# A four-layer Mamba and FFN stack: kernel products of the mixer in adjacent pairs, its output weights loaded a slot ahead, and the closing stage laid out over other banks and engines

## What is computed

```python
# layer 3, per group g of 8, 16 heads of 64 channels, chunks of 128 tokens
M      = einsum('bcihn,bcjhn->bcijh', C, B) * exp(segsum(A*dt))   # 128 x 128 kernels per head
y      = M @ (hid*dt) + (part from the chunk before) + D*hid
yg     = y * silu(gate)
yg     = yg * rsqrt(mean(yg*yg over the group) + eps) * gnorm_w
out    = yg @ out_proj_w.T                                         # 8192 -> 512
# layer 4, blocks of 128, FP8_MAX = 448
def act_quant(x): s = max(|x|)/448 + 1e-12 per token and block; return x/s, s
g, u   = quantised(x) @ w1.T, quantised(x) @ w3.T                  # 512 -> 1792
y      = quantised(silu(g)*u) @ w2.T                               # 1792 -> 512
```

## Time and profile before

| | |
|---|---|
| median of 3 runs | 3027.28 us |
| profiled execution | 3027.26 us |
| its span | 3025.4 us |
| PE busy | 2543.9 us (84%) |
| DVE busy | 1906.6 us (63%) |
| POOL busy | 1276.6 us (42%) |
| ACT busy | 1165.5 us (39%) |
| granted TensorE clock, mean | 0.939 of full |

### The profile page before, as it was taken

The page is one execution under the profiler, slowest core; times in us unless marked ns, Lnnn a source line. Parts: engine busy times, 40 slices in busy tenths (PEclk is TensorE's granted clock), DMA queues, the critical chain, the costliest instruction groups (busy, mean ns, idle before and its releaser), DMA issues. The chain is left out here.

```text
span 3025.4 us, 37783 instructions
## 1 busy us (share of the span) xinstructions
PE 2543.9 (84%) x12700; PEld 1817.9 (60%) x12700; DVE 1906.6 (63%) x2968; ACT 1165.5 (39%) x1935; POOL 1276.6 (42%) x914
## 2 busy tenths in 40 slices
PE   6846667655716999999999999999999999878997
PEld 5611112114615777777777777777777777567886
DVE  4439999985254664565564554655655655487877
ACT  2264444432113553453543543543544534431111
POOL 2109989971002553442543534533534524442212
PEclk9959999997758999999999999999999999889999
DMA  2021030000131110100110100100100101111010
GB/s 72 19 71 43 0 111 0 0 28 28 39 129 54 44 44 23 44 30 23 44 37 16 55 26 23 51 29 23 51 23 24 50 23 37 34 53 39 26 43 29
DMA packets 47743, 116.00 MB, mean 38 GB/s; under 512 B 6560, under 2 KB 6944, under 8 KB 46560
## 3 DMA queue, kind: packets, MB, share of 16 engines
q1 hardware_dynamic: 47584, 113.91, 11.7%
HBM read 104.32 MB, written 9.57 MB: 38 GB/s over the span
## 5 line engine op out<-in xcount | busy, mean ns | idle before, releaser
L1203 POOL TENSOR_TENSOR mg_y<-mg_hT,mg_sg 128x512 f32<-128x512 f32 x128 | 165.4, 1292 | 808.0 <-DVE mg_hT L1453 808.0
L78 PE MATMUL mg_pb<-xT2h,mg_wh 128*128 128x512 f32 x1152 | 464.9, 404 | 15.3 <-POOL mg_wl L1193 15.3
L79 PE MATMUL mg_pb<-xT2l,mg_wh 128*128 128x512 f32 x1152 | 452.5, 393 | 0.0
L80 PE MATMUL mg_pb<-xT2h,mg_wl 128*128 128x512 f32 x1152 | 450.0, 391 | 0.0
L1574 ACT ACTIVATE mg_gb<-mg_gb 128x384 f32<-128x384 f32 x512 | 219.6, 471 | 476.1 <-PE mg_gb L1298 475.9
L743 PE MATMUL ss_y<-ss_pr,cst 128*128 128x512 f32 x512 | 293.2, 661 | 126.4 <-POOL ss_pr L728 116.1
L728 POOL TENSOR_TENSOR ss_pr<-ss_h,ss_bc 128x512 f32<-128x512 f32 x256 | 328.4, 1287 | 38.3 <-DVE ss_h L696 28.5
L1422 DVE SCALAR_TENSOR_TENSOR mg_hT<-mg_pb,mg_cw,mg_hT 128x510 f32<-128x510 f32 (+2 forms) x432 | 318.2, 738 | 34.3 <-ACT mg_hT L1552 32.8
L1446 DVE TENSOR_TENSOR mg_m<-mg_gb,mg_cb 128x384 f32<-128x384 f32 x512 | 270.6, 550 | 43.5 <-ACT mg_gb L1574 33.4
L743 PEld LDWEIGHTS ss_y<-ss_pr,cst 128*128 128x128 f32 x512 | 80.3, 193 | 337.8 <-POOL ss_pr L728 329.4
L78 PEld LDWEIGHTS mg_pb<-xT2h,mg_wh 128*128 128x128 f32 x1152 | 216.8, 188 | 74.3 <-issue 34.9
(11 more groups left out here) (287 smaller groups left out, 5358.5 us busy)
## 6 DMA issues: line engine op xcount, KB each, us to landing
mg_ws<-in_w_in SPq DMA_DIRECT2D x72, 512.0 KB, 3.5
ss_bc<-bc_rows SPq DMA_DIRECT2D x16, 1024.0 KB, 8.8
mg_wos<-in_w_out SPq DMA_DIRECT2D x64, 256.0 KB, 2.6
mg_lr<-acs_rows SPq DMA_DIRECT2D x512, 4.0 KB
ff_ws<-in_w SPq DMA_DIRECT2D x7, 1024.0 KB, 5.0
x<-in_x SPq DMA_DIRECT2D x16, 256.0 KB, 4.1
ip_ws<-in_w_in SPq DMA_DIRECT2D x8, 512.0 KB, 3.3
x_kept<-x SPq DMA_DIRECT2D x2, 2048.0 KB, 7.2
```

Of the source, the lines that this page charges most:

```text
L78: pe.matmul(out, lhs[0], rhs[0], start=start, stop=False)
L79: pe.matmul(out, lhs[0], rhs[1], start=False, stop=False)
L80: return pe.matmul(out, lhs[1], rhs[0], start=False, stop=stop)
L1203: pool.tensor_tensor(yb[:, p % RING, t], hT[s % 2][:, t], sg[s % 2][:, t], ALU.mult).then_inc(s_y2, 1)
```

## The change

In the mixer:
- The landing tile of output weights is doubled (`mg_wos0`, `mg_wos1`), each with its semaphore, and SP issues the loads of slot s+1 at the end of slot s, after the second row loads.
- ScalarE makes the first high weight right after exponential 1 and the second after exponential 5; it copies the high half of the second output tile before exponentials 6 and 7.
- VectorE's products 2 and 3, and 4 and 5, stand next to each other. The low half of the first output tile moves behind the second dt product, that of the second tile ahead of the first skip; the low weights stand ahead of the second dt product and after the last tap of the second half.

In the closing stage:
- Output tiles go to four banks, those of `ff_po` and `ff_pg`; x is transposed into two banks of its own (`tl_px`), three tiles behind the output matmuls instead of two, so that the last three transposes fall in the first three FFN items.
- The scaling of chunk 0's weights moves from GpSimd to ScalarE, as 24 activations of 128 columns; the rounding copies of all chunks are ScalarE's, for chunk f+1 in item 4 of chunk f. GpSimd keeps the subtractions, now in six pieces of 512 columns for each chunk.
- The two broadcast multiplies of `product` become two scalings of 128 columns with two scalars each.

The diff, cut to its core:

```diff
@@ mixer: SP
-                    for w in new_out_weights(s) if s < NSTEP else []:
-                        if w:
-                            sp.wait_ge(s_wgl, w)
-                        sp.dma_start(wos[:], I["w_out1"][w]).then_inc(s_wo, 16)
                     if s == NSTEP:
                         break
                     if more:
                         load_rows(p + 1, 1)
+                    for w in new_out_weights(s + 1):
+                        if w >= 2:
+                            sp.wait_ge(s_wgl, w - 1)
+                        sp.dma_start(wos[w % 2][:], I["w_out1"][w]).then_inc(s_wo[w % 2], 16)
@@ mixer: VectorE
                         kernel_of(p, 1)
+                        if ow:
+                            low_weight(ow[0])
+                        times_step(p, 1)
                         if outs:
                             low(*outs[0])
-                        times_step(p, 1)
                         tap(1, s, 0)
                         kernel_of(p, 2)
+                        kernel_of(p, 3)
                         tap(2, s, 0)
-                        kernel_of(p, 3)
                         tap(3, s, 0)
-                        if ow:
-                            low_weight(ow[0])
                         tap(1, s, 1)
                         kernel_of(p, 4)
+                        kernel_of(p, 5)
                         tap(2, s, 1)
-                        kernel_of(p, 5)
                         tap(3, s, 1)
+                        if ow:
+                            low_weight(ow[1])
                         if outs:
                             add(*outs[0])
+                            low(*outs[1])
                         skip(p, 0)
...
@@ mixer: ScalarE
                             high(*outs[0])
+                        if ow:
+                            high_weight(ow[0])
                         first_tap(s, 0)
                         decay(p, 2)
                         decay(p, 3)
-                        if ow:
-                            high_weight(ow[0])
                         first_tap(s, 1)
                         decay(p, 4)
                         decay(p, 5)
+                        if ow:
+                            high_weight(ow[1])
                         if bc:
                             first_tap(s, 2)
+                        if outs:
+                            high(*outs[1])
                         decay(p, 6)
                         decay(p, 7)
...
@@ closing stage: banks
-        ob = banks(c, "tl_ob", 2)
+        px = banks(c, "tl_px", 2)
         pg = banks(c, "ff_pg", 2)
         pt = banks(c, "ff_pt", 2)
         po = banks(c, "ff_po", 2)
+        ob = po + pg
@@ closing stage: GpSimd
-                scaled(pool, 0, 0)
-                scaled(pool, 0, 1)
-                scaled(pool, 0, 2)
+                def low_part(f, part, piece):
+                    hi_w, lo_w, src = (wh, wl, ws) if part < 2 else (w2h, w2l, w2s)
+                    k = (2 * piece, 2 * piece + 2) if part < 2 else (piece, piece + 1)
+                    pick = (lambda t: t[:, part, k[0]:k[1]]) if part < 2 else (lambda t: t[:, k[0]:k[1]])
+                    i = pool.tensor_tensor(pick(lo_w[f % 2]), pick(src), pick(hi_w[f % 2]).bitcast(F32), ALU.subtract)
+                    if part and piece:
+                        i.then_inc(s_lo, 1)
...
                     add_x(m)
+                    if 2 <= m < 5:
+                        pool.wait_ge(s_hi, 2)
+                        low_part(0, m - 2, 0)
+                        low_part(0, m - 2, 1)
...
+                    for part in range(3):
+                        low_part(f, part, 0)
+                        low_part(f, part, 1)
@@ closing stage: TensorE
-                    if m >= 2:
-                        turn_x(m - 2)
...
+                    if m >= LAG:
+                        turn_x(m - LAG)
+                for n in range(ITEMS):
                     gate_up(n)
+                    if n < LAG:
+                        turn_x(MT - LAG + n)
+                    if n >= 1:
+                        turn_h(n - 1)
+                    if n >= 2:
+                        down(n - 2)
@@ closing stage: ScalarE
+                def scale_up(part):
+                    if part == 0:
+                        act.wait_ge(s_w, 64)
+                    wv, scv = chunk_blocks(0, part)
+                    for b in range(2 * KD):
+                        i = act.activation(wv[:, b], wv[:, b], ACT.Copy, scale=scv[:, b:b + 1])
+                    i.then_inc(s_dq, 1)
+
+                def weights_high(f):
+                    act.wait_ge(s_dq, f * 3 + 3)
+                    if f == 1:
+                        act.wait_ge(s_out, Y0 + MT)
+                    if f >= 2:
+                        act.wait_ge(s_o, (f - 1) * MT)
+                    act.activation(wh[f % 2], ws[:], ACT.Copy).then_inc(s_hi, 1)
+                    act.activation(w2h[f % 2], w2s[:], ACT.Copy).then_inc(s_hi, 1)
+
                 high(0)
                 high(1)
+                scale_up(0)
...
+                    norm_o(m)
+                    if m < 2:
+                        scale_up(m + 1)
+                    if m == 2:
+                        weights_high(0)
+                    if m >= LAG:
+                        x_high(m - LAG)
+                root(1, MT - 1, MT)
+                for n in range(ITEMS):
+                    f, m = divmod(n, MT)
                     silu(n)
+                    if n < LAG:
+                        x_high(MT - LAG + n)
+                    if n >= 1:
+                        h_high(n - 1)
+                    if m == 4 and f + 1 < FC:
+                        weights_high(f + 1)
@@ closing stage: VectorE
-                    ch.link(dve.tensor_tensor(hv, hv, qr[i][:].unsqueeze(2).to_broadcast([P, 2, QB]), ALU.mult))
-                    dve.tensor_tensor(hv, hv, qs[i][:].unsqueeze(2).to_broadcast([P, 2, QB]), ALU.mult
-                                      ).then_inc(s_h, 1)
+                    for b in range(2):
+                        ins = dve.tensor_scalar(hv[:, b], hv[:, b], qr[i][:, b:b + 1], qs[i][:, b:b + 1],
+                                                ALU.mult, ALU.mult)
+                    ins.then_inc(s_h, 1)
...
+                stats_x(MT - 1)
                 for n in range(ITEMS):
                     f, m = divmod(n, MT)
                     product(n)
+                    if n == 0:
+                        quantised(MT - 1)
                     if n >= 1:
                         h_low(n - 1)
                     if n >= 2:
                         add(n - 2)
+                    if n < LAG:
+                        x_low(MT - LAG + n)
```

More of the change, by code:

```diff
@@ L1091, in mixer_groups @@
         wl = [sb(c, f"mg_wl{i}", [P, KD, 2 * P], F32R) for i in range(2)]
-        wos = sb(c, "mg_wos", [P, DM])
+        wos = [sb(c, f"mg_wos{i}", [P, DM]) for i in range(2)]
         yh = sb(c, "mg_yh", [P, PAIRS, P], F32R)
@@ L1514, in _ @@
                         kernel_of(p, 7)
-                        if ow:
-                            low_weight(ow[1])
                         if outs:
-                            low(*outs[1])
                             add(*outs[1])
@@ L1585, in high_weight @@
                 def high_weight(w):
-                    act.wait_ge(s_wo, 16 * w + 16)
+                    act.wait_ge(s_wo[w % 2], 16 * (w // 2) + 16)
                     if w >= PAIRS:
                         act.wait_ge(s_out, w // PAIRS * MT)
-                    act.activation(wogh[:, w % PAIRS, :], wos[:], ACT.Copy, scale=gn[:, w:w + 1]).then_inc(s_wog, 1)
+                    act.activation(wogh[:, w % PAIRS, :], wos[w % 2][:], ACT.Copy, scale=gn[:, w:w + 1]).then_inc(s_wog, 1)
                 def root(g):
@@ L1810, in out_tile @@
                     pe.wait_ge(s_yl, Y0 + m + 1) if m < 2 else pe.wait_ge(s_ylp, m - 1)
-                    if m >= 2:
-                        pe.wait_ge(s_acc, Y0 + m - 1)
+                    if m >= 4:
+                        pe.wait_ge(s_acc, Y0 + m - 3)
                     for k in range(PAIRS):
-                        last = mm3(pe, ob[m % 2][:], (yh[m % 2][:, k, :], yl[m % 2][:, k, :]),
+                        last = mm3(pe, ob[m % 4][:], (yh[m % 2][:, k, :], yl[m % 2][:, k, :]),
                                    (wogh[:, k, :], wogl[:, k, :]), k == 0, k == PAIRS - 1)
@@ L1822, in turn_x @@
                     for k in range(KD):
-                        last = pe.transpose(pt[m % 2][:, k * P:(k + 1) * P], acc[:, m, k * P:(k + 1) * P], ident)
+                        last = pe.transpose(px[m % 2][:, k * P:(k + 1) * P], acc[:, m, k * P:(k + 1) * P], ident)
                     last.then_inc(s_t, 1)
@@ L1855, in down @@
                         pe.wait_ge(s_oacc, n - 1)
+                    else:
+                        pe.wait_ge(s_acc, Y0 + MT - 3 + n)
                     for b in range(2):
@@ L1863, in _ @@
                     out_tile(m)
```

(61 more changed lines are left out.)

67 lines of the change are left out of this document (18 added, 49 removed).

## The result

The changed kernel takes 2943.25 us (median of 4 runs, 2941.93 to 2943.61) against 3027.15 us before on the same chip: ratio 0.972, 95% interval 0.9703 to 0.9736, 83.9 us less. The prediction was 2941. Its profiled execution took 2941.93 us, with a span of 2940.1 against 3025.4: 85.3 us less.

| part | before | after | gained | predicted |
|---|---|---|---|---|
| last mixer slot starts at | 2615.47 | 2569.05 | 46.4 | 47 |
| from there to the gate-up of item 3 | 118.54 | 112.50 | 6.0 | 8 |
| from there to the end | 291.39 | 258.55 | 32.8 | 32 |

A forecast was written before the change was run, and what follows sets the result against it. TensorE was taken to be stopped by order and latency in the mixer, VectorE to bound the output-tile stage. Mixer 47, FFN 32 and output stage 8 sum to 87, less 1 for rounding: 86 off 3027.26, 2941 us, range 2932 to 2949.

The forecast's parts named there:

- Weight slots: Mixer slots loading output weights: earlier weights and adjacent products remove TensorE's wait, 32 x 0.62 = 19.8; term 24 us.
- a hesitation of 0.1 us in 43 slots: Mixer, quiet slots too: small TensorE delay ascribed to product 5, expected to go, about 4.3 us.
- Output slots: Mixer, 21 pair slots: the wait for the second output tile's low half goes, 22.8 us; term 23 us.
- The first low half behind the dt product: Mixer output slots: its new place delays the third segment matmul 0.15 to 0.3 us, 4 us in all; net nothing.
- Rival 3: Mixer: first tile's low half costs 1 us a slot as when locked, 21 us back, time 2962; chance 0.09.
- FFN: Six chunk borders: waits and half clock cost 34 us, 0.3 us a border remains; saved 32, range 24 to 34.
- Rival 1: FFN borders: pieces still hold the product, 1.5 us late at six borders, 9 us, time 2951; chance 0.13.
- Output-tile stage: Closing stage, bound by VectorE: 4.5 + 5.5 - 2 = 8 us gained, range -2 to +14.
- ScalarE: Output-tile stage: 24 scalings estimated at 0.28 each, 6.7 us; sixth tile's low half 2 us late for TensorE, covered by VectorE.
- rival 2: Output-tile stage: ScalarE becomes late, scalings at 0.48; gains nothing or loses 2, time 2949 to 2951; chance 0.12.
- Rival 4: Mixer: output weights come late; landing from 7.1 us on costs 87 us, time 3030 and more; chance 0.03.
- Rival 5: Whole change does nothing: waits only change names as TensorE meets the next late product; 0.03 with the rest.

The follow-up runs named there:

- this one run: Kernel before with only the second output tile's halves moved: ScalarE's high half ahead of exponentials 6 and 7, VectorE's low half behind the first tile's addition; 3001.04 us.
- two moves on VectorE: Changed kernel, mixer: first output tile's low half moved behind kernel product 3, tile 2's taps behind products 6 and 7 in B and C slots; 2935.68 us.
- the end's moves: Changed kernel with item 0's SiLU ahead of the last square root and VectorE's low half between the quantisation's reduction and scale; 2938.5 us.
- whole subtractions: Changed kernel with GpSimd's low halves of the next chunk as whole subtractions instead of pieces, rounding copies still on ScalarE; 2958.98 us.

## Why the prediction came out right

**The total is right partly because errors of single terms cancel.** Of the steps:

- *Weight slots, 24 us: 20.3 measured.* The 19.8 us of true waits were right: by slot lengths the 32 slots gained 20.2, so that the recorded idle time is indeed short of the loss. The 4.3 us for a hesitation of 0.1 us in 43 slots were wrong: it is there in every kernel run, so product 5 does not cause it.
- *Output slots, 23 us: 26.1 by the start of the last slot, 24.7 by the lengths of the 21 slots.* The surplus in the slots was not foreseen: without the wait the output tile behind it takes 5.70 instead of 5.79 us, 21 x 0.09 = 1.9 us, and 22.8 + 1.9 is 24.7. The other 1.4 us lie outside these slots, 0.6 of them in the weight slots of this one run, and are not explained.
- *The first low half behind the dt product.* Predicted 0.15 to 0.3 us a slot; measured 0.11 to 0.18. Moving it again gives it back, so it was this. That the pairs win about as much in these slots was walked rightly too. Rival 3 (1 us a slot, as when locked) is refuted by the 1.28 us the operation takes.
- *FFN, 32 us: 32.8.* In the kernel before the two items at each border are 34.2 us longer over the six borders than twelve quiet ones of 4.45, which is the 34 of the sum. Its parts are a little off: the row's eighth wait, 1.1 us, is that of the last item and not of a border, and the slowed items cost more instead. The walk had the scalings done at +4.6 against a want at +4.42, and a residue of 0.3 us a border. The borders now cost 0.57 at the first and 0.1 to 0.3 at the others. Rival 1 had the scale meet a fresh piece each time, 1.5 us late. The trace shows two held scalings in 2.33 us, one piece each, and the scale held only 0.2 us, by the rest of a piece. The Trainium skill, SBUF — State Buffer, section "Who interferes with whom", has an operation on either side hold the shared port pair to its end; the trace agrees, also for an operation as small as 128x2 (2.44 against 0.17 us).
- *Output-tile stage, 8 us: 6.0.* Here a term was mis-sized. The scalings of quantised tiles were to lose 5 us instead of 9.5, and the sum over the 32 fell from 18.4 to 16.4 us only: 2.0 of the 4.5. The walk had two scalings held in each of two tiles, by a piece each, and nothing behind the pieces. In the trace GpSimd's low half of an output tile stands right behind two pieces. They hold the first two scalings (1.04 and 1.32 us), the low half holds the third (2.46), and only the fourth is free (0.33). In the earlier trace rows one uncut subtraction of 1024 columns holds the first scaling and the same low half the second, so both tiles take 4.92 us: two pieces are as long as what they replace. What was saved is that two tiles are slow and not three (one of the three before took only 2.9). The rest of the stage is a remainder: 6.1 us before the 2.06 us of VectorE's wait for the SiLU are taken off, where 5.5 and 2 had been predicted for the two. Most of it shows behind the gather of tile 7, from where to the first product VectorE takes 9.78 us instead of 14.20, which fits the low halves and the last quantisation that moved to the FFN; no kernel has that move alone. The gather of tile 7 was expected at 65 us into the stage and came at 68.9.
- *ScalarE.* 24 scalings at 0.30 us (0.28 estimated) cost 7.3 us, and the sixth tile's low half comes 2.3 us late for TensorE, as walked. VectorE has no wait for it, so it does not move the end: rival 2 had the mechanism and not the price. The scalings were not put back on GpSimd in any kernel, nor were the four banks tried alone.
- *Rival 4* (weights late) needed a landing at 7.1 us into the slot. The load leaves a slot earlier, and the copy has no wait at all. *Rival 5* (waits only change names) is refuted by the mixer's waits.

## What to carry to other kernels

Before you sum two edits that meet the same wait, compare each with the lateness itself: where one clears the 0.6 us, the second brings nothing there, and both in the sum would have counted the wait twice. A wait on an engine that is not the bound of its stage can come back in full without costing time, so size a stage by the chain of its slowest engine. In an order written by hand look for an operation with slack that stands ahead of one without: two moves on VectorE brought 6.7 us here. Cutting an operation that holds another into pieces helped here at the chunk borders and not at the output tiles, where another long operation stood behind the pieces: list what the holding engine does next.

## What the runs showed of the hardware

Scales and shifts of VectorE on one to four columns are held by GpSimd like large operations. Here are the shift of a tile (two SBUF inputs, one column) beside a low half of GpSimd in the changed kernel, and the same line when GpSimd is idle:

```profile
2606.92 2.40 POOL L1755 TENSOR_TENSOR tl_yl<-mg_y,tl_yh 128x1024 fp32r<-128x1024 f32 x1 [16.98 <-ACT tl_yh L1869]
2607.25 2.08 DVE L1976 SCALAR_TENSOR_TENSOR tl_shift<-tl_mv,tl_inv 128x1 f32<-128x1 f32 x1
...
2640.83 0.16 DVE L1976 SCALAR_TENSOR_TENSOR tl_shift<-tl_mv,tl_inv 128x1 f32<-128x1 f32 x1
```

2.08 us for 0.16 us of work. In the same stretches the statistics, the reductions, the reciprocals and the operations with an input from PSUM keep their usual time (0.69 us for the reduction of 512 columns beside GpSimd's addition of x). These can run beside GpSimd; but as the end's moves show, a held operation moved out of the way of one may meet the next.

A wait of TensorE of 1.9 to 2.3 us left the granted clock at 1.00 (2.4 GHz) in the stretches around five of the six borders with whole subtractions, while the six borders of the kernel before, with waits of 3.7 to 3.9 us, all have 0.76 to 0.88. What else decides it stays open: the sixth border, with a wait of 2.01, has 0.87, and behind a wait of 2.25 us in the output-tile stage of the changed kernel the clock is 0.55 over the next 3.8 us, mostly 1.2 GHz.
